# Second cross-attention of a two-layer decoder: a loop of batch turns replaced by an unrolled table of slots

## What is computed

```
q = (layernorm(x) @ Wq + bq)      16 heads of 16
k = (ctx @ Wk + bk)
v = (ctx @ Wv + bv)
w = softmax(q k^T * 16**-0.5)     512 x 64 a head
x = x + (w v) @ Wo + bo
```

## Time and profile before

| | us |
|---|---|
| median of three runs | 2285.22 (2285.04 to 2290.65) |
| the profiled execution | 2289.26 |
| its span | 2287.7 |
| PE, DVE, ACT, POOL busy over the span | 1738.8, 1382.0, 1080.9, 841.4 |
| second cross-attention, first transfer to end of last bias | 1343.5 to 1709.3 |

### The profile page before, as it was taken

One profiled execution on the slowest core, in us unless ns is written; L12 is line 12 of the kernel. 1 busy time (PEld: TensorE's weight loads), 2 busy tenths in 40 slices (PEclk: granted clock), 3 DMA queues, 4 the chain that ended last, 5 costly groups with the idle time before them and its releaser, 6 DMA issues. The chain is left out here.

```text
span 2287.7 us, 35514 instructions
## 1 busy us (share of the span) xinstructions
PE 1738.8 (76%) x12206; PEld 875.7 (38%) x12222; DVE 1382.0 (60%) x3734; ACT 1080.9 (47%) x1482; POOL 841.4 (37%) x862
## 2 busy tenths in 40 slices
PE   4888888888688865677777745666656887999992
PEld 2122222222355542233333322323323554666661
DVE  2667777773478972566666543535447875555554
ACT  2366766766367962555555411121214563444441
POOL 3235554522477313577776430000002342222221
PEclk8589999999699986799998666668777998999996
DMA  4333332320100003344433014112112333222217
GB/s 95 61 66 61 58 62 50 49 27 1 67 1 1 1 4 56 53 63 57 56 48 48 2 28 58 25 35 38 37 30 95 124 121 106 63 61 61 59 53 234
DMA packets 117853, 126.58 MB, mean 55 GB/s; under 512 B 21684, under 2 KB 104116, under 8 KB 117652
## 3 DMA queue, kind: packets, MB, share of 16 engines
q1 hardware_dynamic: 106980, 101.94, 22.7%
q0 software_dynamic: 6480, 18.23, 2.1%
q10 hardware_dynamic: 4224, 4.19, 0.6%
HBM read 77.94 MB, written 45.16 MB: 54 GB/s over the span
## 5 line engine op out<-in xcount | busy, mean ns | idle before, releaser
L655 ACT ACTIVATE at_pexp<-ps 128x1024 f32<-128x1024 f32 (+3 forms) x480 | 385.8, 826 | 200.5 <-PE ps L888 199.4
L716 DVE TENSOR_REDUCE at_mx<-ps 128x1 f32<-128x512 f32 x512 | 324.0, 683 | 146.3 <-PE ps L895 144.3
L895 PE MATMUL ps<-at_ks,at_qs 48*128 48x512 f16 (+3 forms) x1024 | 291.6, 359 | 95.6 <-DVE at_mx L716 42.4
L182 PE MATMUL ps<-mo_wall,mo_xt 128*128 x1704 | 302.0, 327 | 1.1 <-DVE mo_xt L2316 0.6
L888 PE MATMUL ps<-at_qs,at_ks 50*128 50x512 f16 (+4 forms) x1024 | 253.8, 346 | 29.1 <-DMA at_qs<-at_mhl 23.2
L948 PE MATMUL ps<-at_pexp,at_vaug 128*32 128x512 f32 (+4 forms) x2048 | 226.4, 536 | 7.4 <-issue 6.3
L182 PEld LDWEIGHTS ps<-mo_wall,mo_xt 128*128 128x128 f16 x1704 | 161.1, 98 | 95.2 <-issue 4.3
L2073 POOL DMA_INDIRECT mo_yd<-mo_xn,mo_idu x71 | 68.1, 959 | 272.1 <-DVE mo_xn L2335 266.9
L718 DVE CUSTOM_DVE_ANT_0 at_junk<-ps,at_lmask 128x192 bf16<-128x192 f32 x384 | 115.4, 352 | 80.7 <-PE ps L895 79.6
L895 PEld LDWEIGHTS ps<-at_ks,at_qs 48*128 48x128 f16 x1024 | 75.4, 98 | 213.3 <-DVE at_mx L716 122.6
L888 PEld LDWEIGHTS ps<-at_qs,at_ks 50*128 50x128 f16 x1024 | 70.7, 98 | 174.6 <-issue 88.5
(11 more groups left out here) (397 smaller groups left out, 3873.2 us busy)
## 6 DMA issues: line engine op xcount, KB each, us to landing
at_qs<-at_scratch SPq DMA_DIRECT2D x96, 128.0 KB, 7.2
at_ks<-at_scratch SPq DMA_DIRECT2D x96, 128.0 KB, 7.8
mo_xr<-mo_xs SPq DMA_DIRECT2D x71, 136.0 KB, 2.3
at_scratch<-at_qkh SPq DMA_DIRECT2D x64, 128.0 KB
at_scratch<-at_qkl SPq DMA_DIRECT2D x64, 128.0 KB
x_qs<-x_qscratch SPq DMA_DIRECT2D x48, 128.0 KB
mo_stage<-in_m_gate SPq DMA_DIRECT2D x9, 512.0 KB, 3.7
mo_stage<-in_m_up SPq DMA_DIRECT2D x9, 512.0 KB, 4.6
```

What stands on the lines that cost most here:

```text
L182: last = nc.tensor.matmul(out, lhs, rhs, start=(n == 0), stop=(n == len(terms) - 1))
L655: last = act.activation(columns(pexp[:, U % 2, hh], at, n, stride, width), columns(banks(r, ST[S % 2], 2), at, n, stride, width), ACT.Exp, ...
L716: last = ve.reduce_max(out, score, AX.X)
L895: return nc.tensor.matmul(banks(r, MX[i % 2])[:, piece.at:piece.at + piece.n], qs[rows, (n // 2) % 2, h // 2, piece.idx * P:(piece.idx + 1 ...
```

## The change

The core of the diff:

```diff
-def staggered(eng, nb, turn):
-    turn(0, 0, False, True)
-    turn(1, 1, True, True)
-    with eng.Fori(1, nb // 2 - 1) as k:
...
+CROSS1 = {"STATS": (-29, -26, -22, -15), "RSTD": -17, "APPLY": -12, "XS": -3, "XT": (-9, -6), "Q": (4, 7), "QL": 1, "SAVE": 13, "STACK": 26,
+          "MAX": (42, 46, 48, 49), "MS": 45, "MT": 54, "MHL": 51, "ROWS": 61, "MAIN": (57, 60, 61, 63), "EXP": (61, 61, 66, 67),
+          "AV": (61, 63, 63, 69), "OT": (66, 68, 70, 70), "TO": (73, 76, 78, 82), "Y": (71, 71, 71, 74), "YS": (79, 80), "YT": (90, 90),
+          "OUT": (95, 95), "RES": (92, 93), "BIAS": 94}
+CROSS1_PERIOD = 40
...
+        RINGS = ((("MAX", "MAIN"), (2, 4)), (("XT", "Q", "MT", "YT"), (0, 1)), (("AV", "TO", "OUT"), (6, 7)))
...
+            def split_x(b):
+                pool.wait_ge(norm.xn_ready, b + 1)
+                if b:
+                    pool.wait_ge(xt_done, NC * b)
+                pool.tensor_copy(xsplit[:, 0], norm.xn[:]).then_inc(xsplit_ready, 1)
+                pool.wait_ge(xsplit_ready, 2 * b + 1)
+                pool.tensor_tensor(xsplit[:, 1], norm.xn[:], xsplit[:, 0], ALU.subtract).then_inc(xsplit_ready, 1)
...
+            def low_queries(b):
+                pool.wait_ge(q_ready, NC * (b + 1))
+                if b:
+                    pool.wait_ge(saved, 32 * b)
+                pool.tensor_tensor(ql[:], q32[:], qh[:], ALU.subtract).then_inc(ql_ready, 1)
...
+            for t in range(START, END):
+                for b, k in due(t, "MAIN"):
+                    scores(b, k)
+                for b, j in due(t, "MAX"):
+                    maxima(b, j)
...
```

More of the change, by code:

```diff
@@ L1635, in cross1_phase @@
[L1635 to L1638, removed]
@@ L1694, in turn @@
[L1694 to L1698, removed]
-            save(0)
-            stack(0, 0)
-            staggered(sp, nb, turn)
+                    for q in range(2):
+                        at = 64 * par + 48 + q
+                        sp.dma_start(qs[at:at + 1, b % 2], mhl[q * H + par * NP_:q * H + (par + 1) * NP_, :]).then_inc(rows_in, 16)
+            for t in range(START, END):
+                for b, _ in due(t, "ROWS"):
+                    rows(b)
+                for b, _ in due(t, "SAVE"):
+                    if b == 0:
+                        keys()
+                    save(b)
+                for b, _ in due(t, "STACK"):
+                    stack(b)
@@ new lines, in _ @@
+            for t in range(START, END):
+                for b, j in due(t, "MAX"):
+                    maximum(b, j)
+                for b, j in due(t, "Y"):
+                    shares(b, j)
+                for b, half in due(t, "RES"):
+                    residual(b, half)
+                for b, j in due(t, "STATS"):
+                    statistics(b, j)
+                for b, _ in due(t, "APPLY"):
+                    if b == 0:
+                        prepare()
+                    apply(b)
@@ new lines, in queries, with maxima @@
+            def queries(b, m):
+                pe.wait_ge(xh_ready, NC * (b + 1))
+                emptied(("Q", b, m))
+                product(nc, banks(r, bank["Q", b, m]), [(w, part[:, c, :]) for w, c, part in three("q", m * P, (m + 1) * P, xhl[:, b % 2, 0], xhl[:, b % 2, 1])]).then_inc(q_done, 1)
+            def maxima(b, j):
+                if j == 0:
+                    pe.wait_ge(stacked, 128 * (b + 1))
+                    if b == 0:
+                        pe.wait_ge(kstacked, 16 * NKD)
+                        pe.wait_ge(kh_ready, 1)
+                        pe.wait_ge(v_ready, 1)
+                emptied(("MAX", b, j))
+                for i in range(NP_):
+                    last = nc.tensor.matmul(banks(r, bank["MAX", b, j], 2)[:, i * P:(i + 1) * P], qs[:, b % 2, i, j * P:(j + 1) * P], kst[:, i * B + b, :], start=True, stop=True)
+                last.then_inc(mxs_ready, 1)
```

462 lines of the change are left out of this document (260 added, 202 removed).

## The result

The changed kernel takes 2188.88 us, the median of four runs (2184.24 to 2192.16), against 2285.36 for the kernel before on the same chip: a ratio of 0.9571, with an interval from 0.9546 to 0.9596. The profiled execution took 2192.16 us, 97.1 less than the one of before. Forecast were 2208.2 from a range of 2173 to 2252, so the direction and the range held, and the saving of 96.5 us lies between the 77 of the forecast and the 103 of rival A. The narrower range of the likeliest case, 2194 to 2229, did not hold.

A forecast was written before the change was run, and what follows sets the result against it. Latency of one batch's chain was taken to bound the second cross-attention. First score product at 1394.6, seven periods of 28.5 and a 38.2 us tail end at 1632.3, 77 us less: 2208.2 us, eight in ten 2173 to 2252.

The forecast's parts named there:

- rival A: TensorE's clock is full through the second cross-attention's cycle: 24.8 us a batch, saving 103, 2182 us; chance 0.27.
- likeliest case: Second cross-attention at 28.5 us a batch (26.5 to 31.5): 2208 us, range 2194 to 2229; chance 0.49.
- The tail: Last batch, from its first score product to its bias sum: 38.2 us against 38.5 before, no gain from overlap.
- 1. and 2.: Split, transpose and copy of the maxima, then four row transfers beside the output product: scores start at 6.3 us.
- 3.: Scores to the end of the last value product: 9.2 us, 7.4 at full clock, 10.5 at half.
- 4.: TensorE's eight groups of transposes and score products for maxima, plus two query products: 9.3 us at mean clock 0.8.
- 5.: Two activations of the query products, then GpSimd's subtraction of queries, 2.12: 3.7 us with the hand-over.
- The second ring: GpSimd's queue through output product, residual, bias, rstd, normalisation, split of x: ready at 15.7 us, TensorE there at 15.5.
- rival B: GpSimd's queue or TensorE at half clock bounds the stage: 34.8 us a batch, saving 33, 2252 us; chance 0.19.
- 29.7 case: GpSimd's query subtraction and maxima split, stretched beside VectorE, add 1.2 us a batch, giving 29.7 us a batch.
- rival C: Stacked query rows land late, past 4.6 us of cover, making the kernel slower: at 42 us a batch 2303; chance 0.03.
- Rival D: Single buffers tie batches so a batch stays at 38.9 us, no overlap: 2281 us, within 0.3%; chance 0.02.

The follow-up runs named there:

- two in flight: Changed kernel with a period of 80 slots instead of 40, so only two batches overlap: 2311.77 us, ratio 1.0035.
- bias sum late: Changed kernel with GpSimd's bias addition moved behind rstd and the split of x: 2184.48 us, ratio 0.9557.
- rings of one: Changed kernel in which a bank waits until the unit just before it, not two back, is empty: 2275.29 us, ratio 0.9962.
- QL twice: Changed kernel with GpSimd doing the subtraction of queries a second time into a free buffer: 2207.84 us, ratio 0.9667.
- bias sum twice: Changed kernel with one more GpSimd addition as long as the bias, ahead of rstd and the split of x: 2198.18 us, ratio 0.962.
- statistics early: Late bias addition kernel, with statistics, rstd and normalisation of batch n+2 also moved ahead of the residual: 2196.89 us, ratio 0.9536.
- copies of the products the wrong way: Changed kernel with the copy of the value products moved from ScalarE back to VectorE: 2215.95 us, ratio 0.9693.
- combined kernel: Changed kernel plus late bias, early statistics, row transfers from two queues, filler transposes, and query subtraction behind the maxima split: 2171.07 us, ratio 0.9495.
- the fill: Changed kernel plus twenty unread transposes where TensorE waits for the split of the maxima: 2185.37 us, ratio 0.958.

## Why the prediction was right, and where it was off

**The bound.** Latency of one batch's chain, to be divided among batches in flight: shown. With the same instructions and two in flight the time is 0.35% above that of before, and with up to four it is 4.3% below.

**The start.** First score product forecast at 1394.6, found at 1393.27; 1.05 of the difference is an earlier start of the stage. **The tail.** Forecast 38.2, found 40.4 (1569.85 to 1610.26), from these rows:

```profile
1393.27 1.03 PE L1955 MATMUL ps<-x_kst,x_qs 128*128 128x128 f16 x8 [2.26 <-DMA x_qs<-x_qscratch]
...
1569.85 0.61 PE L1955 MATMUL ps<-x_kst,x_qs 128*128 128x128 f16 x8
...
1607.92 2.34 POOL L1760 TENSOR_TENSOR X<-X,x_bias_out 128x1024 f32<-128x1024 f32 x1 [9.23 <-DVE X L1879]
```

The tail is not free of the batch before: from the first score product to MS it took 6.5 us, not 5.3, because VectorE still had shares of batch 6 to do ahead of the first maximum. The rest, 33.9, varies with the clock. With the bias sum late the same steps took 30.4, with 6.8 us from scores to values where the changed kernel has 9.4.

**The period.** (1569.85 - 1393.27) / 7 = 25.2, forecast 28.5. By its steps:

1. and 2. MS to the start of the scores: 6.3 forecast, 6.19 in the short turns and in the long ones alike. Right, and the output product never ended last (5.9).
3. Scores to the end of the values: 9.2 forecast, 6.75 to 7.76 found. **This term was mis-sized.** The 9.2 was taken from the undisturbed last batch, where the four score matmuls run at 1.2 GHz (1.89 us; 1.04 here at full clock). The bound that I had worked out for full clock, 7.4, lies between the values found. ScalarE's copies between the exponentials cost nothing: with the copies back on VectorE this step took no less, 6.84 at full clock against 6.75.
4. XT to the end of Q: 9.3 forecast, 6.9 in the short turns, 8.0 in the long ones. **Mis-sized as well, mostly by the same assumption**: the mean clock of 0.8 was wrong. Over the ring it was 0.91, and 1.00 in this stretch of a short turn. The hand-overs were too dear as well, for at full clock the sum gives 7.6 and 6.9 was found. (The text's value at half clock, 13 and 1, adds up to 14.0 and not 13.8; nothing hangs on it.)
5. Q to the end of QL: 3.7 forecast, 3.6 found (1.38 from Q's end to QL, 2.12, and 0.1 to MS).

```profile
PE ps L182 <- DVE x_xl L1778: 20.0, 8, 2.5
PE ps L182 <- DVE x_yl L1813: 19.0, 8, 2.4
```

In the changed kernel the halves are made ahead of the transposes, and neither wait is in the list. That alone does not bring the clock back: with two batches in flight these waits are gone too, others stand in their place, and the clock is 0.73. Nor did TensorE run "mostly" at half clock before: between levels of 0.5 and 1.0, means of 0.71 to 0.82 are 42 to 64% of the time at full clock.

**The second ring.** The text put it at 0.2 us from the first: ready at 15.7 against 15.5. In fact both came sooner: ready at 13.35 or 15.0, against 13.9 or 12.9. It did bind, in the two long turns for 2.1 us each and in that of 23.57 for 0.5. From the end of the output product to the split the sum was 8.9, and 9.1 was found; only the product's end was put too late, at 6.8 against 5.9 at the latest. What the text left out are the statistics and the variance behind the residual, 1.7 us. That cost nothing as long as the bias sum of 2.35 us covered them, and it is one reason why moving the bias sum gained 2.3 us of ring instead of 6; the others are above. Its chance, in rival B with half clock, is out: nothing like 34.8 was seen.

**Contention.** I had put GpSimd's QL at 2.12 or, stretched as in the earlier trace rows, more, with P = 29.7. The groups of the stage in the changed kernel show it unstretched, and another instruction stretched instead, the variance on four elements:

```profile
L1851 DVE TENSOR_SCALAR x_var<-x_mv 128x4 f32<-128x4 f32 x8 | 9.1, 1136 | 0.3
...
L1735 POOL TENSOR_TENSOR x_ql<-x_q,x_qh 128x1024 f16<-128x1024 f32 x8 | 17.0, 2123 | 30.2 <-ACT x_q L1800 30.2
```

QL took 2126 ns on average before and 2123 after. That the 29.7 case falls is what the Trainium skill, SBUF — State Buffer, section Who interferes with whom, would have, by the sentence that the prediction takes from it: beside QL VectorE does maxima, which read PSUM, and statistics. I had not looked at the other direction.

**The stacks.** Cover of 4.6 us forecast. The score products waited for stacked rows only ahead of the first batch (2.26 us, above); rival C did not come near. At two in flight, and with everything else shortened, that wait does appear (46.3 and 1.2 us), so the cover was a real quantity and not an infinite one.

**Unrolling** was put at 0 to 1 us a batch. By the run with a period of 80 slots it cannot be separated from the rest; that the stage's 97.9 us stand against 97.1 of the whole profiled execution says that nothing outside the stage was paid for it.

**Rival D** (single buffers tie the batches) is out: no wait of that kind in the list. The depth of the banks can tie them, as the run with rings of one shows.

## What to carry to other kernels

When batches are interleaved through in-order queues, find the cycles through the queues, not the busiest engine: a microsecond on a half-idle engine costs a full one or more if it stands in the cycle (QL twice), and less the more slack there is beside it (bias sum twice). Then look for work of another batch that stands behind a wait of this one and needs nothing from it; moving it ahead is free (bias sum late and statistics early together, 7 us; copies of the products the wrong way, 23 us). And price TensorE's work in the new order at the clock that the new order earns: the more idle time the change removes, the less the clock of the old trace is worth.

## What the runs showed of the hardware

**A four-element VectorE instruction held up by a GpSimd one.** The variance takes 170 ns alone, in the kernel with the late bias sum, and 1509 ns in the combined kernel. Its group in the combined kernel, and the two instructions side by side:

```profile
L1855 DVE TENSOR_SCALAR x_var<-x_mv 128x4 f32<-128x4 f32 x6 | 9.1, 1509 | 0.2
...
1446.29 2.13 POOL L1734 TENSOR_TENSOR x_ql<-x_q,x_qh 128x1024 f16<-128x1024 f32 x1
1446.93 1.51 DVE L1855 TENSOR_SCALAR x_var<-x_mv 128x4 f32<-128x4 f32 x1
```

It ends at 1448.44, 0.02 us after the subtraction that was under way (1448.42). In the changed kernel it is the same beside the bias sum: 1487.65 against 1487.63. The Trainium skill, SBUF — State Buffer, section Who interferes with whom, says that a tensor_scalar can take the shared port pair, and that whoever comes second then stands still until the other's instruction is over. The trace agrees, for an instruction of four elements too. That the cause is the port is the page's word; the runs show only that the two end together, and that the delay is gone where they don't meet.

**The clock behind a short wait.** The same wait of 2.66 us ahead of the transposes of the maxima stands in short and long turns. In the one the 27 matmuls behind it run in 2.85 us, and the 1.2 GHz stretch comes only in the scores; in the other it begins about 1.0 us into the output product (single matmuls go from 0.27 to 0.42 us there, in the timeline). Why it falls in the one place or the other stays open. That the wait is behind the fall in the output product is shown by the fill, which took the clock over the ring from 0.91 to 0.94 and that fall away; the stretches in the scores stayed in some turns.
